# Moving the second half of each projection ahead of the attention transposes, and joining the transposes, in a two-layer graph-attention kernel

## The chip, the cores and the metric

The kernel runs on one core of one Trainium2 chip. The metric is device time in microseconds (us) of one launch. Three runs of the kernel before gave 2176.46, 2176.55 and 2181.41 us; the median is 2176.55 us.

## The reference

The input is `x` (128 graphs of 128 nodes with 256 features) and a 0/1 matrix `adj` for each graph. Two attention layers run one after the other; each has 8 heads of 32 features. Cut to what matters:

```
# layer 0
nx  = layer_norm(x) * g1 + b1
q, k, v = nx@wq + bq, nx@wk + bk, nx@wv + bv
s   = q k^T / sqrt(32) + (0.1*adj*adj where adj > 0, else -inf)
x1  = x + softmax(s) v @ wo + bo
x2  = x1 + gelu((layer_norm(x1)*g2 + b2) @ w1 + b1m) @ w2 + b2m
# layer 1
q, k, v = x2@Wq + bq, x2@Wk + bk, x2@Wv + bv
s   = q k^T / sqrt(32), -inf where adj == 0
out = layer_norm(x2 + softmax(s) v @ Wo + bo) * gamma + beta
```

## The kernel before, in words

Four graphs form a group, so there are 32 groups. A *unit* is one graph in one layer. Each iteration (`Shape`) works on three groups in a software pipeline: stage A is layer 0's attention of one group, stage M is the MLP of the group before it, stage C is layer 1's attention of the one before that. Iterations 0 and 1 fill the pipeline, 2 to 30 are a hardware loop, 31 to 33 drain it (31 still has the shape of a full iteration, without a following group to prepare).

An iteration has eight steps. Step k makes the scores of one unit (steps 0 to 3: units of stage C, steps 4 to 7: of stage A). In the same step the unit of the step before has its softmax probabilities transposed (operation T), and the unit two steps back is multiplied by its values (V, line 1386) and by the output projection (W, line 1395, recorded at line 1233). Beside this, each step holds a piece of dense work in tables made in `Shape`: `early` and `mid` stand ahead of the transposes, `ahead` and `fill` behind them. In steps 0, 1, 2 and 5, 6, 7 the dense work is a projection to keys, queries or values in two halves: the first in `early` or `mid`, the second in `fill`. In step 3 it is the MLP's first matrix (UP 0 to 7) and half of its second (DOWN 0), in step 4 DOWN 1. `ahead` holds XT, the transposes of a group's four residual or normalised blocks (L1266), in steps 2, 4 and 7: their result, split in a high and a low part (ACT L713, DVE L952), is the input of the next dense work.

Nothing is scheduled by a tool: each engine has its own loop over the steps, in written order, and engines meet by semaphores. TensorE (`PE`) does, per step: scores (`make_scores`), V, `early` and `mid`, T of heads group 0 (`turn(t, r, 0)`, four transposes), W, T of heads group 1, `ahead`, `fill`. ScalarE (`ACT`) does: the high part of V's result, the first four exponentials, evacuation of `early`/`mid`, the copy of the first four transposed heads (`turned`, L744), the last four exponentials, then `ahead` and `fill`. VectorE (`DVE`) does: masking of the scores, reciprocals, the low part of V's result, the residual addition of W's result (`add_residual`, L1015), the copy of the last four transposed heads (`turned`, L999), the statistics of the layer norm, `ahead`. GpSimd (`POOL`) multiplies the exponentials by the reciprocals (L615) and adds biases.

Three waits matter. The scores of one unit and the transposed heads share the PSUM tensor `p_heads`, so `make_scores` waits until both copies of the latest T are out of it (L1348 and L1349: `turned_out0`, `turned_out1`). A T waits until its probabilities are made and until the masking has read the same banks (L1363, L1364). A projection waits for the low part of its input, one half of the features after the other (`split_of`, L1295 and L1318). Dense results rotate over four PSUM banks in the order in which `number` counts the operations of a step.

Of the kernel before, what the change touches and what calls it, by code (L numbers as in the profile page):

```python
# [46 lines left out]
NG = B // GB  # L47
# [25 lines left out]
class Shape:  # L73
# [3 lines left out]
    def __init__(self, it, stages, following, before, drain):  # L77
        self.it, self.following, self.before, self.drain = it, following, before, drain
        self.a, self.m, self.c = ("A" in stages), ("M" in stages), ("C" in stages)
        self.units = {k: ("C", k) for k in range(GB)} if self.c else {}  # L80
        if self.a:
            self.units.update({GB + k: ("A", k) for k in range(GB)})
        self.steps = sorted(self.units)
        self.order = [self.units[k] for k in self.steps]
        self.looped = it == "loop"
        self.turns = NG - 3 if self.looped else 1
        pending = before is not None and not before.drain
        self.lag, self.tail = lags(self.steps, pending, drain)


        self.late, waiting = {}, [-3] if pending else []
        for k in self.steps:
            self.late[k] = waiting
            waiting = [r for op, r in self.lag[k] if op == "W"]
        self.last = waiting + [r for _, r in only("W", self.tail)] if drain else []

        self.behind = 3 if self.m else None
        self.open = [k for k in self.steps
                     if ((k - 1 in self.units and k - 1 != self.behind) if k != self.steps[0] else pending)]


        a, m = self.a, self.m
        self.first = {0: [("XT", "A")]} if before is None else {}
        second = before is not None and before.before is None
        self.ahead = {2: [("XT", "M")] * m, 4: [("XT", "C")] * m,
                      7: [("XT", "N")] * (a and following and before is not None)}
        early = {1: ("Q", "A", 0), 2: ("V", "A", 0), 4: ("DOWN", 1), 6: ("Q", "C", 0), 7: ("V", "C", 0)}
        mid = {0: [("K", "A", 0)], 3: [("UP", 0), ("UP", 1)], 5: [("K", "C", 0)]}
        fill = {0: [("K", "A", 1)], 1: [("Q", "A", 1)], 2: [("V", "A", 1)],
                3: [("UP", j) for j in range(2, FC)] + [("DOWN", 0)],  # L110
                5: [("K", "C", 1)], 6: [("Q", "C", 1)], 7: [("V", "C", 1)]}
        present = [k for k in range(STEPS) if (a and not second if k < 3 else m)]
        self.early = {k: [early[k]] for k in present if k in early}
        self.mid = {k: mid[k] for k in present if k in mid}
        self.fill = {k: fill[k] for k in present if k in fill}
        if it == NG:
            for table in (self.mid, self.fill, self.early):
                for k in (5, 6, 7):
                    table.pop(k, None)
            self.tail = self.tail[:3] + [("XH", "C", 0)] + self.tail[3:]  # L120
            self.ahead[4], self.fill[4] = [("KH", "C", 0), ("XH", "C", 1)], [("QH", "C", 0), ("KH", "C", 1)]
        if it == NG + 1:
            self.early[0], self.fill[0] = [("QH", "C", 1), ("V", "C", 0)], [("V", "C", 1)]
        if before is None:

            del self.early[2], self.fill[2]
            self.fill[4] = [("V", "A", 0), ("V", "A", 1)]
            self.early.update({5: [("XT", "N")], 6: [("K", "N", 1)], 7: [("Q", "N", 1)]})
            self.fill[1].append(("BIAS", 1))
            self.fill.update({5: [("K", "N", 0)], 6: [("Q", "N", 0)]})  # L130
            self.fill[7] = [("BIAS", 7)]
            self.tail = self.tail[:1] + [("BIAS", 2), ("V", "N", 0)] + self.tail[1:-1] + [
                ("BIAS", 3), self.tail[-1], ("V", "N", 1)]
        if second:
            self.ahead[2], self.ahead[3] = [("XH", "M", 0)], [("XH", "M", 1)]
            self.mid[3] = [("UH", j, 0) for j in range(3)]
            self.fill[3] = [("UH", 3, 0)] + [("UH", j, 1) for j in range(FC // 2)] + [("DOWN", 0)]

        self.use, self.high = {}, {}
        for k in range(STEPS):  # L140
            lag = self.lag.get(k, [])
            self.number(self.first.get(k, []) + only("V", lag) + self.early.get(k, [])
                        + self.mid.get(k, []) + only("W", lag) + self.ahead.get(k, []) + self.fill.get(k, []))
            if k == self.steps[-1]:
                self.number(self.tail)
        if before is None:
            self.unit0 = self.use0 = self.high0 = 0
        else:
            self.unit0 = before.unit0 + before.turns * len(before.order)
            self.use0 = before.use0 + before.turns * len(before.use)  # L150
            self.high0 = before.high0 + before.turns * len(before.high)
        assert not self.looped or len(self.use) % BANKS == 0
# [8 lines left out]
def only(kind, ops):  # L161
    return [op for op in ops if op[0] == kind]
# [82 lines left out]
def build(nc, T, out):  # L245
    ctx = ExitStack()
    with ctx:
# [551 lines left out]
        def _(dve):  # L799
# [196 lines left out]
            def turned(t, r):  # L996
                u, _, _ = t.unit(r)
                dve.wait_ge(probs_turned, u * KC + 2)
                nc.vector.tensor_copy(turned_rows(1), turned_columns(1)).then_inc(turned_out1, 1)  # L999
# [60 lines left out]
            def body(t):  # L1060
                s = t.s
                setup_over(dve, t)
                for k in range(STEPS):
                    lag = s.lag.get(k, [])
# [21 lines left out]
                    for op in s.early.get(k, []) + s.mid.get(k, []):  # L1086
                        if op[0] == "DOWN":
                            prepare(t, k)
                        if op[0] in ("DOWN", "UP", "UH"):
                            evacuate(t, op)  # L1090
                    for _, r in only("W", lag):
                        add_residual(t, r)
                    for _, r in only("T", lag):
                        turned(t, r)
                    for op in s.early.get(k, []) + s.mid.get(k, []):
                        if op[0] not in ("DOWN", "UP", "UH", "Q", "K"):
                            evacuate(t, op)
# [52 lines left out]
        def _(pe):  # L1150
# [207 lines left out]
            def turn(t, r, g):  # L1358

                u, _, _ = t.unit(r)  # L1360
                par = (r if r >= 0 else r + 8) % 2
                scored = u + 1 if r == len(t.s.order) - 1 and t.s.drain else u + 2
                pe.wait_ge(masked_made, (scored - 1) * H + HC * (g + 1))  # L1363
                pe.wait_ge(probs_made, u * KC + g + 1)  # L1364
                wait(pe, turned_out1 if g else turned_out0, u)
                for n in range(HC):
                    last = nc.tensor.transpose(turned_columns(g)[:, n // 2, (n % 2) * P:(n % 2 + 1) * P],  # L1367
                                               scores[:, par, HC * g + n, :], ident[:, :])
                last.then_inc(probs_turned, 1)
# [29 lines left out]
            def body(t):  # L1399
                s = t.s  # L1400
                setup_over(pe, t)
                for k in range(STEPS):
                    lag = s.lag.get(k, [])
                    for op in s.first.get(k, []):
                        work(t, op)
                        early_products(1)
                    if k in s.units:
                        make_scores(t, k)
                    for op, r in only("V", lag):
                        lagging(t, op, r)  # L1410
                    for op in s.early.get(k, []) + s.mid.get(k, []):
                        work(t, op)
                    for _, r in only("T", lag):
                        turn(t, r, 0)
                    for op, r in only("W", lag):
                        lagging(t, op, r)
                    for _, r in only("T", lag):
                        turn(t, r, 1)
                    for op in s.ahead.get(k, []):
                        work(t, op)  # L1420
                    for op in s.fill.get(k, []):
                        work(t, op)
                    for op in s.tail if k == s.steps[-1] else []:
                        if len(op) == 2 and op[0] in "TVW":
                            lagging(t, *op)
                        else:
                            work(t, op)

            run_pipeline(pe, shapes, body)


# [19 lines left out]
```

## Time and profile before

| | |
|---|---|
| median of 3 runs | 2176.55 us |
| the profiled execution | 2176.37 us |
| its span, first to last instruction | 2174.5 us |
| mean granted TensorE clock | 0.996 |
| PE busy | 2140.2 us, 98% |
| PE weight loads busy | 1854.5 us, 85% |
| DVE busy | 1801.7 us, 83% |
| ACT busy | 1684.7 us, 77% |
| POOL busy | 1154.6 us, 53% |

The execution's time is 1.9 us longer than the span, which is what lies around it. A row of a timeline gives the start, the length, engine, line, operation, what is written from what, and the number of instructions merged into the row; in brackets the idle time before it and who ended that. The length of a row of matmuls reaches to the modelled end of the last one, past the start of the next row, so steps are best read from start to start.

### The profile page before, as it was taken

What the parts mean: (1) busy time and instruction counts of PE and PEld (TensorE: products, weight loads), DVE (VectorE), ACT (ScalarE), POOL (GpSimd) and SP (SyncE); (2) the same over time, 40 slices, a digit from 0 to 9 for tenths busy, and PEclk for the clock granted to TensorE, in tenths of its full rate; (3) what the DMA queues carried; (4) which work ended last, traced back from release to release, by engine and by line L of the source; (5) the groups of instructions that cost most, each with busy time, mean ns of one, the idle gap of its engine ahead of it and who ended that gap; (6) DMA issues with size and microseconds to landing.
All of it is one profiled execution on the core that took longest, in us unless ns stands there. A gap on an engine that the chain in (4) does not pass through costs nothing.

```text
span 2174.5 us, 59064 instructions
## 1 busy us (share of the span) xinstructions
PE 2140.2 (98%) x20372; PEld 1854.5 (85%) x20372; DVE 1801.7 (83%) x8415; ACT 1684.7 (77%) x5658; POOL 1154.6 (53%) x1264
## 2 busy tenths in 40 slices
PE   8899999999999999999999999999999999999997
PEld 6888888888888888888888888888888888888876
DVE  6788888888888888888888888888888888888885
ACT  5677887778787778777787877787877788777875
POOL 4445555545655445655455554456554455554554
PEclk9999999999999999999999999999999999999998
DMA  4100111010111011111101110101110011101000
GB/s 129 33 31 28 38 33 40 29 32 29 40 33 40 24 33 34 38 35 31 33 26 41 33 40 26 35 28 40 34 40 23 28 38 34 39 31 31 19 26 18
DMA packets 94309, 75.76 MB, mean 35 GB/s; under 512 B 8128, under 2 KB 93760, under 8 KB 94016
## 3 DMA queue, kind: packets, MB, share of 16 engines
q1 hardware_dynamic: 94016, 71.99, 10.8%
q8 instruction: 167, 2.74, 0.5%
q14 instruction: 126, 1.03, 0.2%
HBM read 55.20 MB, written 16.78 MB: 33 GB/s over the span
## 4 chain that ended last, share of the span: by engine, by line
PE 96%; DVE 2%; ACT 1%; issue 1%; POOL 0%; DMA 0%; SPq 0%; POOLq 0%; DVEq 0%; ACTq 0%
PE p_bank L1233 67%; PE p_heads L1367 10%; PE p_heads L1354 8%; PE p_bank L1386 7%; PE p_bank L1266 4%; ACT scores L692 1%; DVE probs_t L999 0%; DVE scores L925 0%; DVE normed L952 0%; PE p_bank L1156 0%; DMA scores<-in_L_gnn_wk 0%; DVE x_two L832 0%; SPq L469 0%; DVE normed L946 0%; PE p_heads L1156 0%
## 5 line engine op out<-in xcount | busy, mean ns | idle before, releaser
L692 ACT ACTIVATE scores<-scores,negmax 128x128 f32<-128x128 f32 x2048 | 793.8, 393 | 22.7 <-DVE negmax L925 22.3
L615 POOL TENSOR_TENSOR scores<-scores,inverse 128x512 f32<-128x512 f32 x512 | 542.0, 1064 | 324.9 <-DVE inverse L936 324.9
L692 ACT ACTIVATION_READ_ACCUMULATOR scores<-scores,negmax 128x1 f32 x2048 | 392.1, 191 | 0.0
L1233 PEld LDWEIGHTS p_bank<-w_down,hidden 128*128 128x128 f32 x3072 | 374.6, 190 | 8.5 <-issue 5.9
L1233 PE MATMUL p_bank<-w_down,hidden 128*128 128x256 f32 x3072 | 381.8, 284 | 0.0
L1233 PE MATMUL p_bank<-normed,w_up 128*128 128x512 f32 (+1 forms) x1584 | 369.3, 389 | 3.6 <-DVE normed L946 2.9
L1233 PEld LDWEIGHTS p_bank<-normed,w_up 128*128 128x128 f32 x1584 | 286.2, 188 | 67.0 <-issue 10.2
L1367 PE MATMUL p_heads<-ident,scores 128*128 128x128 f32 x2048 | 310.0, 274 | 7.0 <-DVE negmax L925 4.4
L925 DVE CUSTOM_DVE_ANT_0 scores<-p_heads,adj_a 128x128 f32<-128x128 f32 x1024 | 235.1, 285 | 43.8 <-issue 43.7
L1367 PEld LDWEIGHTS p_heads<-ident,scores 128*128 128x128 f32 x2048 | 239.3, 140 | 32.9 <-DVE negmax L925 12.4
L735 ACT ACTIVATE p_bank<-p_bank,ready_cols 128x512 f32<-128x512 f32 x248 | 164.2, 662 | 126.8 <-PE p_bank L1233 121.5
L925 DVE CUSTOM_DVE_ANT_0 scores<-p_heads,adj_c 128x128 f32<-128x128 f32 x1024 | 233.2, 286 | 31.4 <-issue 31.4
L1233 PE MATMUL p_bank<-w_o,heads_t 128*128 128x256 f32 x1536 | 247.2, 297 | 2.3 <-DVE heads_t L1005 2.3
L749 ACT ACTIVATE heads_t<-p_bank 128x256 fp32r<-128x256 f32 x256 | 98.6, 385 | 161.8 <-PE p_bank L1386 161.8
L986 DVE TENSOR_TENSOR hidden<-p_bank,hidden 128x512 fp32r<-128x512 f32 x248 | 171.5, 691 | 60.7 <-ACT hidden L739 54.8
L744 ACT ACTIVATE probs_t<-p_heads 128x512 f32<-128x512 f32 x256 | 149.7, 585 | 87.2 <-PE p_heads L1367 87.2
L1233 PE MATMUL p_bank<-normed,w_k 128*128 128x512 f32 (+1 forms) x780 | 210.0, 405 | 4.1 <-DVE normed L952 2.6
L1233 PE MATMUL p_bank<-normed,w_q 128*128 128x512 f32 (+1 forms) x780 | 210.9, 406 | 0.0
L560 POOL TENSOR_TENSOR rstd_A<-spread_A,half 128x4 f32<-128x4 f32 x32 | 32.6, 1018 | 331.3 <-DVE spread_A L826 331.2
L1233 PE MATMUL p_bank<-w_v,normed 128*128 128x256 f32 x1536 | 208.4, 285 | 0.0
L1233 PEld LDWEIGHTS p_bank<-w_o,heads_t 128*128 128x128 f32 x1536 | 200.1, 191 | 3.2 <-DVE heads_t L1005 3.0
L1233 PEld LDWEIGHTS p_bank<-w_v,normed 128*128 128x128 f32 x1536 | 185.3, 188 | 12.2 <-issue 12.1
(130 smaller groups left out, 3709.8 us busy)
## 6 DMA issues: line engine op xcount, KB each, us to landing
res_a<-in_x SPq DMA_DIRECT2D x32, 512.0 KB, 3.8
out<-res_c SPq DMA_DIRECT2D x128, 128.0 KB, 1.7
x_in<-in_x SPq DMA_DIRECT2D x31, 512.0 KB, 3.9
adj_a<-in_adj SPq DMA_DIRECT2D x32, 256.0 KB, 2.9
adj_c<-in_adj SPq DMA_DIRECT2D x32, 256.0 KB, 2.8
piece_room<-in_L_gnn_w SPq DMA_DIRECT2D x2, 512.0 KB, 9.0
x_two<-in_x SPq DMA_DIRECT2D x1, 512.0 KB, 6.2
res_c<-in_L_gnn_w SPq DMA_DIRECT2D x1, 512.0 KB, 7.0
```

Of the source, the lines that this page charges most:

```text
L615: nc.gpsimd.tensor_tensor(rows_g, rows_g, inverse[:, step % 2, heads].unsqueeze(2).broadcast_to([P, HC, P]), ALU.mult).then_inc(probs_made, 1)
L692: last = nc.scalar.activation(scores[:, k % 2, h], scores[:, k % 2, h], ACT.Exp, scale=-1.0, bias=negmax[:, k % 2, h:h + 1], accum_out=tot ...
L735: nc.scalar.activation(src[:, :], src[:, :], ACT.Gelu, bias=ready_cols[:, 8 + j:9 + j]).then_inc(gelu_made, 1)
L744: nc.scalar.activation(turned_rows(0), turned_columns(0), ACT.Copy).then_inc(turned_out0, 1)
L749: nc.scalar.activation(heads_t[:, HI].rearrange("p c n -> p (c n)"), p_bank[bank][:, 0:KC * P], ACT.Copy).then_inc(high_made, 1)
L925: nc.vector.tensor_tensor_reduce(out=scores[:, k % 2, slot], in0=score_columns(c, j), in1=adj[stage][:, b, :], scale=1.0, scalar=LARGEST, ...
L986: nc.vector.tensor_tensor(hidden[:, j, LO, :], src[:, :], hidden[:, j, HI, :].bitcast(F32), ALU.subtract).then_inc(drained[bank], 1)
L1233: last = nc.tensor.matmul(dst, stationary(i), moving(j), start=(n == 0), stop=(n == total_n - 1))
L1266: last = nc.tensor.transpose(dst[:, b * P:(b + 1) * P], src[:, b, c * P:(c + 1) * P], ident[:, :])
L1354: last = nc.tensor.matmul(score_columns(c, j), queries[room(t, stage)][rows_j, c, tokens], keys[room(t, stage)][rows_j, c, tokens], start= ...
L1367: last = nc.tensor.transpose(turned_columns(g)[:, n // 2, (n % 2) * P:(n % 2 + 1) * P], scores[:, par, HC * g + n, :], ident[:, :])
L1386: last = nc.tensor.matmul(dst[HD * j:HD * (j + 1), c * P:(c + 1) * P], values[room(t, stage)][:, b, h * HD:(h + 1) * HD], probs_t[:, slot_ ...
```

## The change

In the iterations 1 to 31, in all steps, three things are done. In the steps 0, 1, 2, 5, 6 and 7 the operations of `fill` are appended to `mid`, so that both halves of a projection stand ahead of the transposes, on PE and, since the table is the same, on ACT. PE does both groups of transposes in one run of eight and then W. On DVE the copy of the second group comes before the residual addition. What is in `ahead` (the transposes of residual blocks) so becomes the last of its step. Steps 3 and 4 keep their dense work where it was, and have the other two. Since `number` counts `mid` before W, the banks of the second half and of W change places.

```
+        self.joined = [0, 1, 2, 3, 4, 5, 6, 7] if before is not None and it not in (NG, NG + 1) else []
+        for k in self.joined:
+            if k not in (3, 4) and k in self.fill:
+                self.mid[k] = self.mid.get(k, []) + self.fill.pop(k)
...
(DVE)
+                    if k in s.joined:
+                        for _, r in only("T", lag):
+                            turned(t, r)
                     for _, r in only("W", lag):
                         add_residual(t, r)
-                    for _, r in only("T", lag):
-                        turned(t, r)
+                    if k not in s.joined:
+                        for _, r in only("T", lag):
+                            turned(t, r)
...
(PE)
                     for _, r in only("T", lag):
                         turn(t, r, 0)
+                        if k in s.joined:
+                            turn(t, r, 1)
                     for op, r in only("W", lag):
                         lagging(t, op, r)
                     for _, r in only("T", lag):
-                        turn(t, r, 1)
+                        if k not in s.joined:
+                            turn(t, r, 1)
                     for op in s.ahead.get(k, []):
                         work(t, op)
```

TensorE, step 0 of a full iteration, before: scores of a unit of stage C (L1354), V (L1386), the keys' projection in two halves (`w_k0`), transposes (L1367) and output projection (`w_o0`).

```order
L1354 MATMUL p_heads<-keys_c,queries_c 128x128 x8
L1386 MATMUL p_bank2<-probs_t,values_a 32x128 x8
L1233 MATMUL p_bank3<-normed0,w_k0 128x512 x6
L1367 MATMUL p_heads<-ident,scores 128x128 x4
L1233 MATMUL p_bank0<-w_o0,heads_t 128x256 x6
L1367 MATMUL p_heads<-ident,scores 128x128 x4
L1233 MATMUL p_bank1<-normed0,w_k0 128x512 x6
L1354 MATMUL p_heads<-keys_c,queries_c 128x128 x8
```

The same step now (PE's lines are 9 further down):

```order
L1363 MATMUL p_heads<-keys_c,queries_c 128x128 x8
L1395 MATMUL p_bank2<-probs_t,values_a 32x128 x8
L1242 MATMUL p_bank3<-normed0,w_k0 128x512 x6
L1242 MATMUL p_bank0<-normed0,w_k0 128x512 x6
L1376 MATMUL p_heads<-ident,scores 128x128 x8
L1242 MATMUL p_bank1<-w_o0,heads_t 128x256 x6
L1363 MATMUL p_heads<-keys_c,queries_c 128x128 x8
```

The second half of the projection moved from behind the transposes to ahead of them, and the next scores now stand directly behind the output projection.

TensorE, from step 2's values (`w_v0`) to the first two blocks of the MLP (`w_up`) in step 3, before; `x_two` are the residual blocks of XT:

```order
L1233 MATMUL p_bank3<-w_v0,normed0 128x256 x12
L1367 MATMUL p_heads<-ident,scores 128x128 x4
L1233 MATMUL p_bank0<-w_o1,heads_t 128x256 x6
L1367 MATMUL p_heads<-ident,scores 128x128 x4
L1266 MATMUL p_bank1<-ident,x_two 128x128 x2
L1266 MATMUL p_bank2<-ident,x_two 128x128 x2
L1266 MATMUL p_bank1<-ident,x_two 128x128 x2
L1266 MATMUL p_bank2<-ident,x_two 128x128 x2
L1233 MATMUL p_bank3<-w_v0,normed0 128x256 x12
L1354 MATMUL p_heads<-keys_c,queries_c 128x128 x8
L1386 MATMUL p_bank0<-probs_t,values_c 32x128 x8
L1233 MATMUL p_bank1<-normed1,w_up 128x512 x6
```

And now:

```order
L1242 MATMUL p_bank3<-w_v0,normed0 128x256 x12
L1242 MATMUL p_bank0<-w_v0,normed0 128x256 x12
L1376 MATMUL p_heads<-ident,scores 128x128 x8
L1242 MATMUL p_bank1<-w_o1,heads_t 128x256 x6
L1275 MATMUL p_bank2<-ident,x_two 128x128 x2
L1275 MATMUL p_bank3<-ident,x_two 128x128 x2
L1275 MATMUL p_bank2<-ident,x_two 128x128 x2
L1275 MATMUL p_bank3<-ident,x_two 128x128 x2
L1363 MATMUL p_heads<-keys_c,queries_c 128x128 x8
L1395 MATMUL p_bank0<-probs_t,values_c 32x128 x8
L1242 MATMUL p_bank1<-normed1,w_up 128x512 x6
```

Twelve matmuls of the values' projection no longer stand between the XT and the work that reads it. Step 7 is built alike, with `x_in` and the next iteration's keys.

## Rows read from the trace of the kernel before

**Rows 1.** The page's first part: busy time, share, instructions.

```profile
PE 2140.2 (98%) x20372; PEld 1854.5 (85%) x20372; DVE 1801.7 (83%) x8415; ACT 1684.7 (77%) x5658; POOL 1154.6 (53%) x1264
```

**Rows 2.** The chain that ended last, by engine.

```profile
PE 96%; DVE 2%; ACT 1%; issue 1%; POOL 0%; DMA 0%; SPq 0%; POOLq 0%; DVEq 0%; ACTq 0%
```

**Rows 3.** Timeline of PE, step 0 of one looped iteration: start us, us, instructions.

```profile
1031.32 0.73 PE L1354 MATMUL p_heads<-keys_c,queries_c 32*128 32x128 f32 x16
1031.98 0.64 PE L1386 MATMUL p_bank<-probs_t,values_a 128*32 128x128 f32 x16
1032.55 1.65 PE L1233 MATMUL p_bank<-normed,w_k 128*128 128x512 f32 x6
1034.04 0.60 PE L1367 MATMUL p_heads<-ident,scores 128*128 128x128 f32 x4
1034.39 0.96 PE L1233 MATMUL p_bank<-w_o,heads_t 128*128 128x256 f32 x6
1035.19 0.60 PE L1367 MATMUL p_heads<-ident,scores 128*128 128x128 f32 x4
1035.55 1.64 PE L1233 MATMUL p_bank<-normed,w_k 128*128 128x512 f32 x6
1037.12 0.73 PE L1354 MATMUL p_heads<-keys_c,queries_c 32*128 32x128 f32 x16
```

**Rows 4.** Timeline of PE, step 2 and the start of step 3.

```profile
1042.91 0.73 PE L1354 MATMUL p_heads<-keys_c,queries_c 32*128 32x128 f32 x16
...
1046.78 0.60 PE L1367 MATMUL p_heads<-ident,scores 128*128 128x128 f32 x4
1047.22 1.04 PE L1266 MATMUL p_bank<-ident,x_two 128*128 128x128 f32 x8
1048.01 1.62 PE L1233 MATMUL p_bank<-w_v,normed 128*128 128x256 f32 x12
...
1050.79 3.03 PE L1233 MATMUL p_bank<-normed,w_up 128*128 128x512 f32 x12
1053.65 0.60 PE L1367 MATMUL p_heads<-ident,scores 128*128 128x128 f32 x4
```

**Rows 5.** Timeline of PE and DVE, end of step 4, where no `fill` stands.

```profile
1011.47 0.60 PE L1367 MATMUL p_heads<-ident,scores 128*128 128x128 f32 x4
...
1011.90 1.04 PE L1266 MATMUL p_bank<-ident,x_two 128*128 128x128 f32 x8
1012.10 0.69 DVE L999 COPY probs_t<-p_heads 128x512 f32<-128x512 f32 x1
...
1012.94 0.73 PE L1354 MATMUL p_heads<-keys_a,queries_a 32*128 32x128 f32 x16
```

**Rows 6.** Timeline of PE, last iteration: 24 matmuls of a values' projection unbroken.

```profile
2143.89 2.89 PE L1233 MATMUL p_bank<-w_v,normed 128*128 128x256 f32 x24
2146.71 0.73 PE L1354 MATMUL p_heads<-keys_c,queries_c 32*128 32x128 f32 x16
```

**Rows 7.** Timeline of ACT and DVE, step 2, from the copy to the split input.

```profile
1046.59 0.58 ACT L744 ACTIVATE probs_t<-p_heads 128x512 f32<-128x512 f32 x1
...
1048.61 1.07 ACT L713 ACTIVATE normed<-p_bank 128x512 fp32r<-128x512 f32 x2
...
1049.22 1.29 DVE L952 TENSOR_TENSOR normed<-p_bank,normed 128x512 fp32r<-128x512 f32 x2 [0.37 <-ACT normed L713]
```

**Rows 8.** Timeline of PE, iteration 32: XT and UP with no `fill` between.

```profile
2102.92 1.04 PE L1266 MATMUL p_bank<-ident,x_two 128*128 128x128 f32 x8
...
2105.97 3.00 PE L1233 MATMUL p_bank<-normed,w_up 128*128 128x512 f32 x12 [0.71 <-DVE normed L952]
```

**Rows 9.** Waits over the whole span: us in total, times, longest us.

```profile
PE p_heads L1354 <- DVE probs_t L999: 4.3, 4, 1.7
```

**Rows 10.** Two stretches of iteration 32: us, busy by engine, granted clock, DMA.

```profile
2095.00:2100.00 5.00, 3.94 (x42) 3.27 (x35) 4.16 (x26) 3.94 (x18) 2.19 (x3) 0.70 0.01 3
2100.00:2105.00 5.00, 4.45 (x73) 3.76 (x70) 4.48 (x29) 4.32 (x19) 3.11 (x4) 1.00 0.00 0
```

## The prediction, as it was written before the changed kernel ran

> **What bounds the kernel now.** I read the page's first part, the chain that ended last, and then PE's timeline of one looped iteration. The reader should see that PE is busy for 98% of the span [rows 1] and carries 96% of the chain [rows 2], and that in the timeline its rows follow each other without a bracket, that is, without a wait. So the time is the sum of PE's start-to-start distances. Step 0 runs from scores to scores in 1037.12 - 1031.32 = 5.80 us [rows 3]. Therefore a change of PE's order is worth two things: what the distances become when neighbours change, and whether a wait appears that the old order covered. The cover is what I looked for next, in the places where the old order already has none: the end of step 4, the last iterations, and the list of waits.
>
> **Where the order gains.** A run of matmuls that is broken costs more than one unbroken. Step 0 has six matmuls of 512 columns to the transposes in 1.49 us (1032.55 to 1034.04) and six to the scores in 1.57 us (1035.55 to 1037.12), 3.06 together [rows 3]; twelve in a row, to a transpose, take 1053.65 - 1050.79 = 2.86 us [rows 4]. So joining a projection saves 0.20 us. For the values' projection 24 matmuls to the scores take 2.82 us [rows 6]; scores instead of transposes cost 0.08 more (1.57 against 1.49), so 2.74 to a transpose.
>
> **Where it gains nothing.** Four transposes followed by something else take 0.35 us (1034.04 to 1034.39), but four followed by further transposes take 0.44 (1046.78 to 1047.22), and eight followed by a projection 0.79 (1047.22 to 1048.01) [rows 3, 4]. Two separate fours cost 0.35 + 0.36 = 0.71, so eight in a row are 0.08 dearer. W to its follower is 0.80 (1034.39 to 1035.19) [rows 3]; before scores I take 0.88.
>
> The Trainium skill has a rule by which joining would save nothing ("TensorE: Matmul & The Clock Gate", section "Back-to-back issue gap": columns / 2.4 GHz + 2.5 ns for each matmul, with no term for the end of a run; the section gives a second, lower figure for a stream with weight loads, also without such a term). By it six matmuls of 512 columns take 1.29 us wherever they stand. The row shows 1.49, and twelve take less than twice as much, so the trace does not agree here; the rival below has its price.
>
> **Steps 0, 1, 5 and 6: the copy of the second transposes.** Scores may not start until DVE has copied the last four transposed heads out. Before, the second half of the projection (1.57 us) stood between; now W alone does. The price of that copy is seen at the end of step 4: transposes at 1011.47, their end at 1012.07, the copy at 1012.10 for 0.69, the scores at 1012.94 [rows 5]. That is 1.47 us from the first of these four transposes to the scores; XT to the scores is 1.04 there, against 0.79 to the projection in step 2 [rows 4], so the scores do wait. In the new order the second four start 0.44 behind the first. Scores to scores is then 0.66 (scores to V, 1031.32 to 1031.98) + 0.57 (V to projection) + 2.86 + 0.44 + 1.47 = 6.00 us. PE alone would need 0.66 + 0.57 + 2.86 + 0.79 + 0.88 = 5.76, so 0.24 us of the step is a new wait. Against 5.80 each such step is 0.20 longer. There are 2 x 31 steps (5 and 6) and 2 x 30 (0 and 1): 122 x 0.20 = +24.4 us.
>
> The copy on ACT does not come later than that on DVE. ACT must first evacuate the second half of the projection, which ends 0.16 behind the transposes' start (1.65 long, 1.49 to the next start [rows 3]); the evacuation and the copy are some 0.6 each, so it ends near 1.4, and DVE's near 1.04 + 0.03 + 0.69 = 1.76 (the end of eight transposes is 1.04 [rows 4]). Its last four exponentials now come behind both evacuations; what reads them, the second four transposes of the next step, stands some 6 us later. What queues behind DVE's copy is the residual addition (it waits for W, which ends about when the copy does), the statistics, and then the next masks, some 0.3 us later than now. ACT's exponentials start from the masks' first half but also behind V's high part, so this is absorbed. In step 0 a normalisation stands ahead of the copy too; it could be 0.1 us late, which I keep for the range.
>
> **Steps 2 and 7: XT without cover.** XT's result passes ACT (high part) and DVE (low part) before the next dense work reads it. Before, twelve matmuls covered this. From scores to UP is 1050.79 - 1042.91 = 7.88 us [rows 4]. Now, counted from the first transpose of the eight: W starts at 0.79, XT at 1.59. ACT evacuates the values and is at its copy near 0.70; from that copy to the high part it is 1048.61 - 1046.59 = 2.02 (copy and four exponentials), so the high part starts at 2.72, which is behind XT's first result; the low part starts 0.61 later (1049.22 - 1048.61) [rows 7], at 3.33; half of the 1.29 for two is 0.65, and from a copy's end to PE it is 0.15 (1012.79 to 1012.94 [rows 5]). The dense work starts at 4.13. The whole is 0.66 + 0.57 + 2.74 + 4.13 = 8.10, 0.22 longer than 7.88. Both steps occur 30 times (iteration 31 has no XT in step 7, iteration 1 none in step 2): 60 x 0.22 = +13.2 us. What bounds this from below: if PE alone counted, XT to UP were 0.87 + 0.66 + 0.57 = 2.10 instead of 2.54, and the step 7.66, 0.22 shorter than now. From above: in iteration 32, with nothing between, XT to UP is 2105.97 - 2102.92 = 3.05 with 0.71 of it idle [rows 8], which makes the step 8.61, 0.73 longer. There ACT came late for other reasons; I take 2.54, the chain of the looped iteration.
>
> **Steps 3 and 4.** Step 3 keeps its cover; transposes and W take 0.79 + 0.80 instead of 0.35 + 0.80 + 0.36, so +0.08, 30 times: +2.4. The banks that UP takes next are drained well before. In step 4 the copy now ends before XT does, so the wait of 1.04 - 0.87 = 0.17 goes; but the keys' projection behind it needs XT's low part, for which DVE must be through residual and statistics. Between 0 and -0.17 I take -0.08: -2.4 us.
>
> **Queues moved past.** SP has no new work; its load of `x_in` waits for XT's low part, 0.9 us later in a step where it has several steps to land. POOL's order is unchanged, and the bank rotation gives no operation a bank drained later than one step back.
>
> **Sum.** 24.4 + 13.2 + 2.4 - 2.4 = +37.6 us on the profiled execution's 2176.4 us (span 2174.5 and 1.9 around it; the median of runs, 2176.55, is the same within 0.2): 2214 us.
>
> **The rivals.**
> *PE alone counts (faster).* Copy and split are hidden in fact: the scores find `p_heads` free after W, and UP its input. This decides if DVE's copy is out 0.88 us after W starts. Then 122 x (5.76 - 5.80) - 60 x 0.22 + 2.4 - 30 x 0.17 = -4.9 - 13.2 + 2.4 - 5.1 = -20.8: 2156 us. For it: 98% busy [rows 1], and in steps 0 to 3 DVE's copy never shows as a wait. Against it: the 1.04 of step 4 [rows 5], and the copy's 0.69 cannot start before the transposes end.
> *DVE is late at the copy.* Four times in the draining iterations the scores waited for this copy, 4.3 / 4 = 1.08 us each, 1.7 at most [rows 9]. If masks that come later make DVE late in steps 0 and 1, where normalisations stand in front, the wait there is 1.08 instead of 0.24: 60 x 0.84 = +50 on my sum, 2264 us. For it: DVE is at 83% [rows 1]. Against it: near 1 us of room by my count.
> *Joining saves nothing.* Twelve matmuls take 3.06 - 0.08 = 2.98: 182 x 0.12 = +22 on the sum, 2236 us. Against it: the 2.86 itself [rows 4].
> *The clock falls.* The granted clock was 0.70 from 2095 to 2100 [rows 10], after waits of over 1 us. The loss there is about 0.30 x 5.0 = 1.5 us; once in each of 30 iterations this is +45 on the sum, 2259 us. Against it: the new waits are 0.24 and 0.44 us, and from 2100 to 2105, where PE is busy for 4.45 of 5.00 us and so idle for 0.55, it is 1.00 [rows 10].
> The skill's section on "A second HAM failure mode: psum-queue depth-cycling" (same page) tells of short idle times between groups of matmuls that make the clock swing; by it this last rival would be likely. The trace shows a fall only behind the longer waits.
> *The order does not change what it says:* excluded, it is in the rows of the two orders.
>
> **How the numbers follow.** The forecast 0.74, PE alone 0.08, something between that makes no difference 0.04, DVE late 0.07, joining saves nothing 0.04, the clock 0.03. The likeliest one's own range is 2202 to 2230 (0.1 us either way in the 122 steps). The range that should hold 8 in 10 is 2195 to 2240: half the wait gone at the low end, the bound of rows 8 for half of steps 2 and 7, or no saving, at the high end. Within 0.3% is about what a measurement of this kernel can tell from no change. Faster by more: 0.08; within: 0.04; slower: 0.88.
>
> **What the profile after would show.** PE's scores with a wait on DVE's copy near 0.25 us, some 120 times in total near 30 us; scores to scores in step 0 near 6.00; twelve matmuls to transposes 2.86, the eight 0.79; UP in step 3 and the keys in step 0 waiting for the low part near 0.4 us; the granted clock still above 0.99. Wrong would be: scores to scores at 5.76 with no wait (then the copy is faster than I read it), or DVE's copy starting later than the transposes' end (then DVE has less room than I counted), or UP without a wait.

## The result: 2.4% slower, 2230.9 us

The changed kernel takes 2230.86 us (median of 4 runs, 2228.06 to 2232.92) against 2178.17 us for the kernel before on the same chip: ratio 1.024, 95% interval 1.0227 to 1.0254. The prediction was 2214 us, from 2195 to 2240. The sign, the mechanism and the range hold; the loss is 53 us where 38 was forecast. The profiled execution took 2229.81 us, its span 2228.0 us, so 53.5 us more than before.

The page's first part and the engines of the chain, after (against [rows 1, 2]):

```profile
PE 2153.8 (97%) x20372; PEld 1878.7 (84%) x20372; DVE 1818.7 (82%) x8415; ACT 1687.3 (76%) x5658; POOL 1157.0 (52%) x1264
```

```profile
PE 76%; ACT 11%; DVE 10%; issue 2%; POOL 0%; DMA 0%; SPq 0%; POOLq 0%; DVEq 0%; ACTq 0%
```

The busy shares hardly moved, but the chain did: PE carried 96% of it before, now 76%; the rest now runs mostly through ACT and DVE. The waits of PE over the whole span show for what (us in total, times, longest):

```profile
PE p_heads L1363 <- DVE probs_t L1004: 24.9, 127, 1.1
PE p_bank L1242 <- DVE normed L957: 21.7, 64, 1.5
```

Scores on the copy were 4.3 us in 4 waits before [rows 9]. The second line is the keys and UP, waiting for XT's low part; before, it was:

```profile
PE p_bank L1233 <- DVE normed L952: 3.3, 4, 1.5
```

Step 0 of one iteration, PE and DVE (against [rows 3]):

```profile
1059.83 3.00 PE L1242 MATMUL p_bank<-normed,w_k 128*128 128x512 f32 x12 [0.30 <-DVE normed L957]
1062.67 1.03 PE L1376 MATMUL p_heads<-ident,scores 128*128 128x128 f32 x8
1063.46 0.95 PE L1242 MATMUL p_bank<-w_o,heads_t 128*128 128x256 f32 x6
1063.74 0.69 DVE L1004 COPY probs_t<-p_heads 128x512 f32<-128x512 f32 x1
...
1064.58 0.73 PE L1363 MATMUL p_heads<-keys_c,queries_c 32*128 32x128 f32 x16 [0.17 <-DVE probs_t L1004]
```

Twelve matmuls take 2.84 us, eight transposes 0.79, then 1.12 from W (the output projection) to scores; DVE's copy starts 1.07 behind the first transpose and the scores come 1.91 behind it, as forecast. The brackets understate a wait, since the rows of matmuls reach to their modelled ends: read it from start to start.

Step 2 and the start of step 3, PE, ACT and DVE (against [rows 4, 7]):

```profile
1003.98 3.10 PE L1242 MATMUL p_bank<-w_v,normed 128*128 128x256 f32 x24
...
1006.92 1.03 PE L1376 MATMUL p_heads<-ident,scores 128*128 128x128 f32 x8
...
1007.61 0.59 ACT L749 ACTIVATE probs_t<-p_heads 128x512 f32<-128x512 f32 x1
...
1008.51 1.03 PE L1275 MATMUL p_bank<-ident,x_two 128*128 128x128 f32 x8
...
1009.47 0.73 PE L1363 MATMUL p_heads<-keys_c,queries_c 32*128 32x128 f32 x16
1009.63 1.07 ACT L718 ACTIVATE normed<-p_bank 128x512 fp32r<-128x512 f32 x2
...
1010.24 1.29 DVE L957 TENSOR_TENSOR normed<-p_bank,normed 128x512 fp32r<-128x512 f32 x2 [0.24 <-ACT normed L718]
...
1011.08 1.17 PE L1242 MATMUL p_bank<-normed,w_up 128*128 128x512 f32 x4 [0.30 <-DVE normed L957]
```

From the first transpose: ACT's copy at 0.69, the high part at 2.71, the low part at 3.32, UP at 4.16. The forecast had 0.70, 2.72, 3.33 and 4.13. But the transposes themselves start 2.94 behind the projection's start, where I had 2.74.

Where the time went, from the start-to-start distances of all iterations in both traces (us, sums over the steps of a kind; from scores to scores). "V to keys" and "V to UP" are the distances from the product with the values to the dense work that reads XT's result:

| steps | number | before | after | difference |
|---|---|---|---|---|
| 1 and 6 (queries) | 61 | 354.0 | 366.7 | +12.7 |
| 0 and 5 (keys) | 60 | 351.8 | 373.7 | +21.9, of it 11.8 from V to keys (11.3 in step 0, 0.5 in step 5) |
| 2 and 7 (values) | 60 | 398.7 | 401.8 | +3.1 |
| 3 (MLP) | 30 | 593.5 | 606.6 | +13.1, of it 11.3 from V to UP |
| 4 | 30 | 291.3 | 289.3 | -2.0 |

That is 48.8 of 53.5 us. Of the rest, 1.85 us lie before the first changed step (the scores of the step ahead of it start at 79.90 instead of 78.05), 1.6 in step 5 of the first changed iteration, and about 1 in the draining iterations. Ahead of the projection of that step 5 PE waited twice, 1.60 and 0.63 us, as in the kernel before, but the granted clock was then 0.57 from 90 to 94 us, so mostly at the lower of its two levels (1.2 GHz), against 1.00 before:

```profile
90.00:94.00 4.00, 3.45 (x9) 2.78 (x10) 2.97 (x22) 2.33 (x10) 1.64 (x2) 0.57 0.39 128
```

Over all the steps of the table the granted clock is 1.00 (2.4 GHz), before and after.

### The profile page after: what moved, and what is told of

Same layout as the page of the kernel before. It is cut to its first block, busy times and chain, and to the rows that moved or that the text cites. A ratio compares the mean times of both kernels' runs of the same rounds, so it can differ in the third digit from the quotient of the medians.

```text
span 2228.0 us, 59064 instructions
## 1 busy us (share of the span) xinstructions
PE 2153.8 (97%) x20372; PEld 1878.7 (84%) x20372; DVE 1818.7 (82%) x8415; ACT 1687.3 (76%) x5658; POOL 1157.0 (52%) x1264
## 3 DMA queue, kind: packets, MB, share of 16 engines
q8 instruction: 167, 2.74, 0.5%
## 4 chain that ended last, share of the span: by engine, by line
PE 76%; ACT 11%; DVE 10%; issue 2%; POOL 0%; DMA 0%; SPq 0%; POOLq 0%; DVEq 0%; ACTq 0%
PE p_bank L1242 56%; ACT scores L697 7%; PE p_heads L1376 7%; PE p_heads L1363 6%; PE p_bank L1395 5%; DVE probs_t L1004 4%; DVE normed L957 3%; DVE x_two L837 2%; ACT normed L718 1%; ACT probs_t L749 1%; PE p_bank L1275 1%; ACT values_c L727 1%; ACT values_a L727 1%; DVE scores L930 0%; DMA scores<-in_L_gnn_wk 0%
## 5 line engine op out<-in xcount | busy, mean ns | idle before, releaser
L1004 DVE COPY probs_t<-p_heads 128x512 f32<-128x512 f32 x256 | 176.7, 690 | 211.6 <-PE p_heads L1376 207.5
L1376 PE MATMUL p_heads<-ident,scores 128*128 128x128 f32 x2048 | 270.5, 274 | 6.6 <-DVE negmax L930 3.5
L1242 PE MATMUL p_bank<-normed,w_k 128*128 128x512 f32 (+1 forms) x780 | 195.1, 399 | 13.8 <-DVE normed L957 11.8
L1242 PE MATMUL p_bank<-w_v,normed 128*128 128x256 f32 x1536 | 197.7, 285 | 0.0
L1242 PE MATMUL p_bank<-normed,w_q 128*128 128x512 f32 (+1 forms) x780 | 194.4, 398 | 0.0
```

The costliest lines, as they stand in the source:

```text
L1242: last = nc.tensor.matmul(dst, stationary(i), moving(j), start=(n == 0), stop=(n == total_n - 1))
```

## The experiments

The theory at this point: two waits cost the time, that of scores on VectorE's copy (steps 0, 1, 5, 6), and that of keys and UP on XT's low part (steps 2 and 7). Rivals: W followed by scores is dear on PE itself; one delay is handed from step to step; the eight transposes are the loss.

**Parts of the change alone.**

```
e1: self.joined = [0, 1, 5, 6] if ...
e2: self.joined = [2, 7] if ...
e3: if k in ():                       # no fill is moved
        self.mid[k] = ...
```

> The change made in steps 0, 1, 5 and 6 alone; steps 2, 3, 4 and 7 as before. Theory (two separate costs: the scores' wait for VectorE's copy in these four steps, and XT without cover in steps 2 and 7): the four steps are 0.21 us longer each as in the changed kernel, 122 x 0.21 = +25 us on 2177: about 2202, with scores waiting 120 times near 0.17 us on VectorE's copy and no wait of UP or keys on the low part. Rival (the loss is one thing, PE's order as a whole, or a delay that is handed on from step to step): the four steps alone cost far less than 25 us or nearly all 53.

Measured 2201.97 us against 2178.38, ratio 1.0112 (1.0094 to 1.0131): +23.6. A queries step is 6.00 us on average, a keys step 6.05 (5.80 and 5.86 before). The waits are as the theory has them, and the one on the low part is back at the 3.3 us in 4 waits of the kernel before:

```profile
PE p_heads L1363 <- DVE probs_t L1004: 25.4, 126, 1.7
PE p_bank L1242 <- DVE normed L957: 3.3, 4, 1.5
```

> The change made in steps 2 and 7 alone. Theory: from scores to the next dense work these are 0.43 to 0.45 us longer, 60 x 0.44 = +26 us: about 2203, UP and the keys' projection waiting near 0.3 us each on VectorE's low part; of the 0.44 about 0.1 is the pace inside the 24 matmuls. Rival (the delay comes from ACT and DVE that are late from steps 0, 1, 5, 6): with those steps as before, the wait is gone and the time within 8 us of before.

Measured 2212.90 us, 1.0159 (1.0144 to 1.0174): +34.5, more than the 26 expected. V to UP is 0.95, as in the changed kernel, so that wait needs no delay from other steps: the handing-on rival falls there. But step 0 hands something on that the changed kernel does not. From its second six key matmuls to the scores of step 1 it is 1.96 us (1.57 before): DVE is at the copy only 1.5 us after its transposes start, because a normalisation (`x_two`, 1.21 us) and the residual addition stand ahead of it.

```profile
1051.31 0.66 PE L1376 MATMUL p_heads<-ident,scores 128*128 128x128 f32 x4
1051.39 1.21 DVE L837 TENSOR_SCALAR x_two<-res_a,moments_M,rstd_M 128x256 f32<-128x256 f32 x1
1051.72 1.64 PE L1242 MATMUL p_bank<-normed,w_k 128*128 128x512 f32 x6
...
1052.52 0.41 DVE L1020 TENSOR_TENSOR res_a<-p_bank,res_a 128x256 f32<-128x256 f32 x1
1052.85 0.68 DVE L1004 COPY probs_t<-p_heads 128x512 f32<-128x512 f32 x1
...
1053.68 0.73 PE L1363 MATMUL p_heads<-keys_c,queries_c 32*128 32x128 f32 x16 [0.32 <-DVE probs_t L1004]
```

That is 30 x 0.39 = 12 us. With 11.3 from V to keys and 10.4 in step 3, and 0.9 gained in the values' steps, it accounts for 33. A late low part makes DVE's masks of step 0 late, and what stands behind them; the old order of step 0 has the last transposes out 0.7 us sooner than the joined one. So the parts do not add: 23.6 + 34.5 is 58, the whole change 53.

> The eight transposes in one run ahead of W and VectorE's copy ahead of the residual addition in all steps, but the second half of every projection stays behind them as before. Theory (cover is what was lost): no wait of scores or UP; only eight transposes at 0.79 us instead of 0.71, some 0.08 x 7 x 30.5 = +17, less 2 in step 4: about 2192. Rival (the joined transposes and the copy's new place are themselves the loss): near 2231. Rival (joining is free): 2177.

Measured 2202.52 us, 1.0112 (1.0095 to 1.0129): +24.1, and expected +15 for another reason. A queries step is 5.82 us against 5.80: the 0.08 of eight transposes comes back, because six matmuls to the scores take 1.49 us behind W and 1.57 behind transposes. Nearly all is in one place, step 5 (+21.6 us; steps 2 and 7 have +3.7, step 4 has -2.0), where the second four transposes come 0.7 us sooner than before and find the masks not made. DVE makes them behind XT's low part of step 4:

```profile
1026.26 1.29 DVE L957 TENSOR_TENSOR normed<-p_bank,normed 128x512 fp32r<-128x512 f32 x2
...
1028.56 0.60 PE L1376 MATMUL p_heads<-ident,scores 128*128 128x128 f32 x4
...
1029.71 0.65 PE L1376 MATMUL p_heads<-ident,scores 128*128 128x128 f32 x4 [0.55 <-DVE negmax L930]
...
1030.12 0.96 PE L1242 MATMUL p_bank<-w_o,heads_t 128*128 128x256 f32 x6
```

T to W is 1.56 there instead of 0.79: 30 x 0.77 = 23 us. In the changed kernel the second half of the projection, moved ahead, is what covers this. Neither rival holds, and my theory had not this wait.

**The copy.** In e4 PE signals after six of the eight transposes too, and DVE copies in two parts (the part of the edit on DVE):

```
...
+                for p in range(2):
+                    dve.wait_ge(probs_turned, u * 3 + 2 + p)
+                    nc.vector.tensor_copy(turned_rows(1)[:, p:p + 1], turned_columns(1)[:, p:p + 1]).then_inc(turned_out1, 1)
...
```

> The changed kernel, with VectorE's copy of the last four transposed heads in two parts, the first as soon as two of them are transposed. Theory: the copy's end, not PE's order, holds the scores; it comes about 0.2 us earlier, so W to scores falls from 1.12 towards 0.9: 122 x 0.16 = -20 us, about 2211. Rival (W followed by scores costs 1.1 us on PE by itself): unchanged at 2231. Rival (a copy of 256 columns is not much shorter than one of 512, fixed cost): W to scores longer than 1.12, time above 2231.

Measured 2207.93 us, 1.0136 (1.0116 to 1.0157): 23 us less than the changed kernel. A queries step, PE and DVE:

```profile
1053.07 1.04 PE L1377 MATMUL p_heads<-ident,scores 128*128 128x128 f32 x8
1053.86 0.95 PE L1243 MATMUL p_bank<-w_o,heads_t 128*128 128x256 f32 x6
1053.93 0.76 DVE L1005 COPY probs_t<-p_heads 128x256 f32<-128x256 f32 x2 [1.11 <-PE p_heads L1377]
1054.83 0.73 PE L1364 MATMUL p_heads<-keys_c,queries_c 32*128 32x128 f32 x16
```

In steps 1, 5 and 6 W to scores is 0.965 on average, instead of 1.12. The whole order of PE is the same, so W before scores is not dear on PE: the copy's end held them. Step 0 is different, with 1.09 us. There the same normalisation as in e2 stands ahead of the copy, which so starts 0.99 us behind the transposes' start and not 0.86:

```profile
1046.95 1.21 DVE L837 TENSOR_SCALAR x_two<-res_a,moments_M,rstd_M 128x256 f32<-128x256 f32 x1
1047.88 0.95 PE L1243 MATMUL p_bank<-w_o,heads_t 128*128 128x256 f32 x6
1048.08 0.74 DVE L1005 COPY probs_t<-p_heads 128x256 f32<-128x256 f32 x2
1048.96 0.73 PE L1364 MATMUL p_heads<-keys_c,queries_c 32*128 32x128 f32 x16
```

So the earlier copy is worth 91 x 0.155 + 30 x 0.035 = 15 us, not the 20 expected. About 5 us more lie in the pace of long runs of matmuls, which differs from trace to trace, and the rest outside the table's steps; that the total came out near the forecast is partly luck.

In e5 the transposes are two fours again, with W between, behind the whole projection:

```
                         turn(t, r, 0)
-                        if k in s.joined:
-                            turn(t, r, 1)
...
-                        if k not in s.joined:
-                            turn(t, r, 1)
+                        turn(t, r, 1)
```

> The second half of each projection ahead of the transposes as in the changed kernel, but the transposes again in two fours with W between. Theory: the last four transposes then start 0.35 + 0.80 = 1.15 us behind the first, so scores come at 1.15 + 1.47 = 2.62 instead of 1.91: with 0.66 + 0.57 + 2.86 the step is 6.71 us, 0.7 longer than in the changed kernel: 122 x 0.7 = +85 us, some 2316. Rival (the scores' wait is not tied to the transposes' end): within 10 us of 2231.

Measured 2346.47 us, 1.0761 (1.0741 to 1.078): +167 on the kernel before. A queries step is 6.72 us, as computed (6.71), with 1.47 from the second four to the scores, as in all of the steps 0, 1, 5 and 6; the rows are of step 5:

```profile
1023.27 3.00 PE L1242 MATMUL p_bank<-normed,w_k 128*128 128x512 f32 x12 [0.50 <-DVE normed L957]
1026.11 0.60 PE L1376 MATMUL p_heads<-ident,scores 128*128 128x128 f32 x4
1026.46 0.95 PE L1242 MATMUL p_bank<-w_o,heads_t 128*128 128x256 f32 x6
1027.26 0.60 PE L1376 MATMUL p_heads<-ident,scores 128*128 128x128 f32 x4
1028.73 0.73 PE L1363 MATMUL p_heads<-keys_a,queries_a 32*128 32x128 f32 x16 [0.88 <-DVE probs_t L1004]
```

Of the 30 us beyond my 85, 25 are that V to keys and V to UP grew to 1.14 each (from 0.95, and in step 5 from 0.70): DVE now has the later copy ahead of residual, statistics and low part. I had left DVE's own queue out of this step.

**The low part of XT.** e6 puts XT ahead of W on PE in steps 2 and 7 (with the banks counted in that order), e7 puts XT's high parts ahead of the last four exponentials on ACT:

```
e6 (PE)
+                    if k in s.joined and k in (2, 7):
+                        for op in s.ahead.get(k, []):
+                            work(t, op)
                     for op, r in only("W", lag):
...
e7 (ACT)
+                    early_xt = k in s.joined and k in (2, 7)
+                    for op in s.ahead.get(k, []) if early_xt else []:
+                        evacuate(t, op)
                     if k in s.units and k != s.behind and not long:
                         exps(t, k, 1)
...
```

> The changed kernel, with XT ahead of W in steps 2 and 7, so 0.80 us earlier on PE. Theory (ACT's four exponentials, which stand ahead of XT's high part, set its start): the high part starts as before, UP and keys start no earlier in the step, 2231 within 5 us. Rival (XT's place on PE sets it): UP and keys no longer wait: 60 x 0.3 = -18, about 2213.

Measured 2258.70 us, 1.0361 (1.0347 to 1.0375): 28 us more than the changed kernel, where I expected nothing and the rival a gain.

```profile
1022.87 1.04 PE L1276 MATMUL p_bank<-ident,x_two 128*128 128x128 f32 x8
...
1023.66 0.96 PE L1243 MATMUL p_bank<-w_o,heads_t 128*128 128x256 f32 x6
...
1024.66 0.42 DVE L1021 TENSOR_TENSOR res_c<-p_bank,res_c 128x256 f32<-128x256 f32 x1 [0.89 <-PE p_bank L1243]
1024.71 1.06 ACT L719 ACTIVATE normed<-p_bank 128x512 fp32r<-128x512 f32 x2
...
1025.12 0.43 DVE L824 BATCH_NORM_STATS2 stats_C<-res_c 128x6 f32<-128x256 f32 x1
...
1025.87 1.28 DVE L958 TENSOR_TENSOR normed<-p_bank,normed 128x512 fp32r<-128x512 f32 x2
...
1026.70 2.08 PE L1243 MATMUL p_bank<-normed,w_up 128*128 128x512 f32 x8 [0.85 <-DVE normed L958]
```

The high part does start no earlier, as I said. But DVE's queue has the residual addition and the statistics ahead of the low part, and these wait for W, which now comes 0.9 us later. V to keys and V to UP are 1.49, against 0.95. So the low part starts 1.2 us behind the high part instead of 0.6. In the changed kernel this second chain was ready only 0.24 us ahead of ACT's: DVE stood idle for that long before the low part, waiting for the high one. These steps also give the price of W before scores on PE alone: with the copy out some 0.8 us before the scores start, it is 0.89 us, against the 1.12 of the other steps.

> The changed kernel, with XT's high parts ahead of ACT's last four exponentials in steps 2 and 7. Theory: the high part is then held by XT's end on PE instead, about 0.25 us earlier; UP and keys wait that much less: 60 x 0.25 = -15, about 2216, unless VectorE's statistics (which end near the same time) take over, then -5 to -10. Rival: ACT's exponentials, pushed back by 1 us, make the next step's transposes or scores wait: above 2231.

Measured 2221.52 us, 1.0191 (1.0177 to 1.0205): 9.3 less. V to keys (step 0) and V to UP fall to 0.70 from 0.95, which is the 0.25 and 15 us expected. Most of it is given back one step later:

```profile
1007.22 0.37 ACT L754 ACTIVATE heads_t<-p_bank 128x256 fp32r<-128x256 f32 x1
1007.62 0.42 DVE L1013 TENSOR_TENSOR heads_t<-p_bank,heads_t 128x256 fp32r<-128x256 f32 x1
...
1009.02 0.60 PE L1379 MATMUL p_heads<-ident,scores 128*128 128x128 f32 x4
1009.46 0.29 DVE L933 CUSTOM_DVE_ANT_0 scores<-p_heads,adj_c 128x128 f32<-128x128 f32 x1
...
1009.81 0.66 PE L1379 MATMUL p_heads<-ident,scores 128*128 128x128 f32 x4 [0.19 <-DVE negmax L933]
```

ACT reaches V's high part of step 3 behind the exponentials, DVE's low part follows it, the masks follow that, and the eight transposes take 1.20 us instead of 0.79: 30 x 0.41 = 12 us. The four exponentials did hold XT's high part, and moving them moves the wait. The two leave 3 of the 9.3 us; another 2 to 3 are the pace of the long runs, and the rest lies outside the table's steps.

**A version put together from the parts.** e8 is the change in steps 0, 1, 4, 5 and 6 with the copy in two; e9 is the kernel before with the copy in two:

```
e8: self.joined = [0, 1, 4, 5, 6] if ...     (and e4's edit)
e9: self.joined = [] if ...                  (and e4's edit)
```

> The change made in steps 0, 1, 4, 5 and 6 alone, with VectorE's copy in two parts as in e4. Theory (sum of the measured parts): a step of queries is 5.85 us as in e4 against 5.80 before, 122 x 0.05 = +6; step 4 is 0.07 shorter, -2; steps 2, 3 and 7 as before: about 2183, within 0.4% of before. Rival (the parts act together): far above, where steps 2 and 7 pick up what the others hand on, 2195 or more.

Measured 2182.51 us over 11 runs against 2179.53, 1.0013 (1.0004 to 1.0022). The queries step is 5.85 us, step 4 is 9.64 instead of 9.71, and W to scores is 0.965 in step 0 too, since the low part of step 7 is no longer late. The parts add up here, and the joined order is within 0.2% of the old one once the copy is nearly covered; it does not beat it.

> The kernel before with only VectorE's copy of the last four transposed heads in two parts. Theory: in the old order only step 4 and the draining iterations wait for this copy, so -0.07 x 30 and some tenths in the drain: 2175 to 2178, no difference that can be measured. Rival (the second copy's fixed cost, on an engine busy for 83%, shows): 2183 or more.

Measured 2176.27 us over 12 runs, 0.9989 (0.9978 to 1.0): 0.1% less, with an interval that reaches to no difference, so no clear gain over the kernel before. Step 4 is 0.04 us shorter. No version beat the kernel before by more than the measurement tells.

## Why the prediction was right, and where it was short

**Steps 0, 1, 5 and 6: right.** Forecast +24.4. The table gives +12.7 for queries and 21.9 - 11.8 = +10.1 for keys, 22.8 together, of which the distances agree to hundredths (2.84 to 2.87 for twelve matmuls, 0.79, 1.91 from transposes to scores). e1 gives +23.6, and e4 shows that the copy's end is the cause. In step 0 it is a near thing: DVE is free just when the transposes end (copy 1.07 behind their start in every one of these steps), and e2 and e4 show it late there.

**Steps 3 and 4: right and small.** +2.4 forecast, 13.1 - 11.3 = +1.8 measured; -2.4 forecast for step 4, -2.0 measured, and +0.5 from V to keys in step 5 behind it.

**Steps 2 and 7: the mechanism right, one term mis-sized.** Forecast +13.2; measured 3.1 + 11.3 + 11.3 = +25.7. The chain from the first transpose to UP was right to 0.03 us. The term that failed is "so 2.74 to a transpose" for 24 matmuls of values: it measured 2.91 on average, 0.17 more, 60 x 0.17 = 10 of the 12.5 us missed. Of the 0.17, 0.10 is the neighbour. I had taken the 2.82 of [rows 6] as the price of a joined run. That run stands in the last iteration directly behind other projection matmuls, and its first matmul takes 0.12 us to the second; in the loop it stands behind V, and the first alone takes 0.22. The deduction of 0.08 for transposes instead of scores held: the last matmul takes 0.21 to scores and 0.12 to transposes.

The other 0.07 is the pace, and it is not settled. Inside the joined runs most matmuls of 256 columns are 0.118 us apart and in some iterations 0.113, in one and the same kernel, so the run takes 2.93 or 2.84; of the 60 runs 46 were at the slower pace. In the kernel before the halves were at about 0.114 in every iteration of the loop. In e7 and e2 all take 2.83 to 2.85. What sets it is open; it is worth 4 us here.

Joining did save on PE here as well. Before, the first half took 1.48 us to a transpose and the second, which starts at 1048.01 in [rows 4], 1.55 to the scores, 3.03 together:

```profile
1044.15 1.65 PE L1233 MATMUL p_bank<-w_v,normed 128*128 128x256 f32 x12
1045.63 0.60 PE L1367 MATMUL p_heads<-ident,scores 128*128 128x128 f32 x4
...
1049.56 0.73 PE L1354 MATMUL p_heads<-keys_c,queries_c 32*128 32x128 f32 x16
```

Joined they take 2.84 at the faster pace, 0.19 less, which is what 512 columns gain (3.06 to 2.86), and 2.93 at the slower, 0.10 less.

**The rivals.** PE alone (2156) is excluded by the waits. "DVE is late at the copy" did not occur in the changed kernel, but it did in step 0 of e2 and, by 0.12 us, of e4. "Joining saves nothing" is false for both widths. The clock's rival occurred once, in the first changed iteration, not in every one: the mean granted clock is 0.994 against 0.996. The fall there came in e1 and e5 too, but not in e4, e6 and e7, which have the same waits ahead of it, so the change alone does not bring it; whether it makes it likelier stays open.

**Missed in the sum:** the first iterations, 1.85 us before any changed step and 1.6 with the clock. The first is no effect of the change: up to there the kernels do the same work, and that stretch is 2.1 us shorter in the trace of e4 than in that of the kernel before and 5.8 longer in e6's. A single execution's time carries that much from ahead of the first changed step, which is why the account above goes by steps.

## What to carry to other kernels

When an order that interleaves dense work with small dependent work is untangled, each piece of dense work that leaves its place was a cover: list what sat behind it (here a copy out of shared PSUM, and the split of an input), and add the engine's start-to-start distance from the producer to the waiting instruction. Follow the whole queue of the engine that makes the release, not only its last instruction: e6, and a part of e5, were missed because the residual and the statistics stood ahead of the low part on DVE. A price for a run of matmuls is good only with the same neighbour ahead of it as in the place where it will be used.

## What the runs showed that I had not expected

- Two halves of a projection gain by joining: at 512 columns 1.49 + 1.57 us become 2.84 to 2.87, at 256 columns 1.48 + 1.55 become 2.84 or, in most iterations of the changed kernel, 2.93.
- Six matmuls of 512 columns to scores take 1.49 us behind W and 1.57 behind transposes (e3), so a cost of eight transposes in one run (0.79 against 0.71) comes back at the next run.
- A copy of 2 x 256 columns takes 0.74 to 0.76 us on DVE, against 0.69 for 512 at once: the split costs 0.05 us or a little more there, and its first part runs beside the last transposes.
- Short waits in most steps did not lower the granted clock: in e5 they show as 0.50 and 0.88 us, and it was 1.00 over all looped steps (0.995 over the whole span).
